# Four graph layers over 128 small graphs on one core: double-width instructions, the middle norm folded into G, scores spread by a repeated column, and new step orders

## The chip, the cores and the metric

One NeuronCore of a Trainium2 chip runs the whole program. The metric is device microseconds of one execution. Engines are named as in the profile: PE (TensorE), DVE (VectorE), ACT (ScalarE), POOL (GpSimd), SP (the queue that issues the DMAs).

## The reference, cut to what matters

`x` is [128 graphs, 128 nodes, 256], `adj` is [128, 128, 128], about a quarter of it nonzero. Every layer starts with a layer norm over the 256 features and a relu, and adds its result to `x`:

```
H = (adj != 0);  w = adj's first row;  Dn = 1/(H w);  Be = 1/(column sums of H)        # layer 0, hypergraph, 256 -> 512 -> 256
conv(v, W) = Dn * H @ (Be * (H^T @ (v @ W^T))) + b
x += conv(layer_norm(relu(conv(h, W1))) * gamma + beta, W2) + h
A = max(H, I);  dinv = rsqrt(row sums of A)                                             # layer 1, GCN
x += tanh(dinv * A @ (dinv * h) @ W + b)
s = (h @ w) @ a;  E = exp(leaky(8 * tanh((s_i + s_j) / 8)));  E *= adj                  # layer 2, attention
x += (E / rowsum(E) * rowsum(adj)) @ h @ w
x += adj @ (relu(adj @ (relu(adj @ h @ W1 + b1)) @ W2 + b2)) @ W3 + b3                  # layer 3, three GCN steps
```

## The kernel before, in words

The 128 graphs are worked in 16 passes (`GROUPS`). In a pass four streams A to D each hold J = 2 graphs. Each engine runs a list of steps per pass, `run` at L185, in an order made from the slot tables at L48 to L64: a table gives each step a place, stream B's steps stand a quarter of a pass after A's, C's a quarter after B's, and so on; a step whose place exceeds a pass is carried out in the next turn of the engine's loop (`back` = -1). So the steady state repeats the same pattern every quarter of a pass, with the streams rotated. Every engine works its list strictly in order; semaphores carry the dependences. The loop over passes is a hardware loop on each engine (`Fori`, L198).

Each layer is two kinds of products. A **U step** (`unit`, L300: 0U, 1U, 2U, 3U, 4U, 5U, 6U) multiplies by the graph's matrix (G for layer 0, AT for the GCN, AE for the attention, T = adj transposed for layer 3), in fp32, 128 columns at a time. ACT copies the result to UHI, rounded to fp32r (`take`, L375, step of the same name), and DVE forms the remainder ULO = U - UHI (`low`, L577). A **W step** (`weigh`, L315: 0W to 6W) multiplies by the weights, which are also split: per chunk of 128 features ULO x WHI, UHI x WLO, UHI x WHI, all fp32r, 256 columns wide (512 in 0W). Both graphs of a stream are handled by a loop over `j`: own PSUM bank, own instruction on ACT and DVE, own count on the semaphore. In 4W and 5W a first product adds the bias: SHARES (64 rows) x BIAS (64 rows), L329.

U steps and G and 3S rotate over two pairs of PSUM banks (`UB`), W steps over two pairs (`WB`); `bank_free` at L282 makes PE wait until the step that had the bank is read out.

The other steps that matter here:
- P, PT, P2 (DVE, L535 to L575): statistics of X, HT = (adj^T != 0) with counts, degrees from R = adj, and the small reciprocals after G. G = HT x [BHT | weights | 1] (`g_and_sums`, L336).
- 0W on DVE (`hidden`, L587) scales and adds the bias into Z (512 wide), ACT takes relu (L441), 0N gathers statistics of Z, POOL makes scale and shift, and ACT applies both to Z (0Z, `hidden_scale`, L446) before 1U.
- A norm is `stats` on DVE (L523: two `bn_stats`, a sum at L531, two `bn_aggr`), `norm` on POOL (L710: four or five instructions on 2 columns, one of them a power, L717) and `normalise` on ACT (L384).
- Attention: node scores on DVE (2S, L617), then ACT and DVE make the high and low part of a diagonal matrix of the scores (2D, L429 and L626), PE multiplies ones by it (3S, L345), ACT takes tanh and exp (L421, L436), DVE leak, product with T and row sums (L635 to L653).
- POOL: AT from HT (L727), the rest RES = TMP + X + B2 + H (L743, three instructions per graph), 2A (L766), X3 (L783).
- SP: X of the next pass is loaded after `rest_ready`, T and R after `p6U` (L213 to L224), outputs are stored after `c6W`.

Of the kernel before, what the change touches and what calls it, by code (L numbers as in the profile page):

```python
# [6 lines left out]
F32 = mybir.dt.float32  # L32
# [6 lines left out]
HALF = 32  # L39
TINY = 1.1754944e-38  # L40

PE_SLOTS = {  # L48
    "G": 2.890, "0U": 3.256, "0W": 3.665, "1U": 4.986, "1W": 5.422, "2U": 7.425, "2W": 7.801, "3S": 9.193,
    "3U": 9.672, "3W": 10.446, "4U": 11.122, "4W": 11.483, "5U": 12.384, "5W": 12.888, "6U": 13.845, "6W": 14.116}  # L50
ACT_SLOTS = {
# [3 lines left out]
DVE_SLOTS = {  # L55
# [3 lines left out]
POOL_SLOTS = {  # L59
    "P": 2.7, "AT": 6.2, "DI": 3.3, "R": 4.6, "0N": 5.2, "1W": 7.1, "2A": 8.4, "2X": 8.9, "2S": 9.5, "3W": 11.3,  # L60
    "X3": 12.8}
SP_SLOTS = {
    "X": -0.8, "T": 0.8, "O": 13.2}
SLOTS = 12  # L64


def ordered(slots):


    entries = []  # L70
# [10 lines left out]
def program(nc, xs, adj_t, adj_r, w1t, w2t, l1w, l2w, l2wt, l3w1, l3w2, l3w3,  # L81
            cols, b1, b2, l1b, l3b1, l3b2, l3b3, out):
# [6 lines left out]
    with ExitStack() as ctx:  # L89
# [744 lines left out]
```

## Time and profile before

| what | value |
|---|---|
| runs of the kernel | 1560.72, 1558.03 and 1559.4 us; median 1559.4 |
| profiled execution | span of its trace 1559.0 us; it has no separate time, so its span is its time here |
| busy: PE, DVE, ACT, POOL | 1491.9, 1429.5, 1156.2, 1048.1 us |
| granted TensorE clock, mean | 0.996 of full speed |
| DMA | 35 GB/s over the span, 10.9% of the 16 engines' time |

Reading it: the profile cuts the span in 40 slices, and apart from the first and last the slices look alike, because 16 equal passes run in a steady state. What a change is worth is therefore read in one quarter of a pass, multiplied by four and by the passes, with the start and the end looked at by themselves.

### The profile page before, as it was taken

The numbers are of one execution on the slowest core, as the hardware profiler recorded it, in microseconds if no ns is written. First come the engines' busy times: TensorE is split into PE (matmuls) and PEld (weight loads), VectorE is DVE, ScalarE is ACT, GpSimd is POOL, SyncE is SP. The second block draws the span as 40 slices with busy tenths as digits, with TensorE's granted clock in tenths as the row PEclk, the third lists the DMA queues.
The fourth block names the chain that finished last, engine by engine and source line by source line (L and its number), as shares of the span: only waits on it lengthen the run. The fifth ranks groups of instructions, "written<-read, shape, count | busy, mean of one in ns | idle before, by whom it ended". The sixth has DMA issues, their size and how long they took to land. (4 is left out here: it accounts for less than half of the span.)

```text
span 1559.0 us, 38399 instructions
## 1 busy us (share of the span) xinstructions
PE 1491.9 (96%) x10892; PEld 1369.1 (88%) x10892; DVE 1429.5 (92%) x5145; ACT 1156.2 (74%) x3080; POOL 1048.1 (67%) x2387
## 2 busy tenths in 40 slices
PE   5799999999999999999999999999999999999997
PEld 4798898998989989888988989989899898889896
DVE  6899899999999989999999999999899999999995
ACT  4677777777777777777777777777777787777774
POOL 3767666766767767677676667667677676766762
PEclk8999999999999999999999999999999999999999
DMA  4001101101101001011011011011011010110100
GB/s 152 1 29 35 42 27 34 41 24 37 38 23 41 34 28 41 28 34 41 27 34 41 27 34 41 27 34 41 21 41 34 27 41 28 34 41 27 34 21 21
DMA packets 39119, 54.76 MB, mean 35 GB/s; under 512 B 4464, under 2 KB 21488, under 8 KB 39024
## 3 DMA queue, kind: packets, MB, share of 16 engines
q1 hardware_dynamic: 39024, 53.89, 10.9%
q14 instruction: 84, 0.69, 0.1%
q8 instruction: 11, 0.18, 0.0%
HBM read 37.10 MB, written 16.78 MB: 35 GB/s over the span
## 5 line engine op out<-in xcount | busy, mean ns | idle before, releaser
L381 ACT ACTIVATE UHI_D<-UB 128x256 fp32r<-128x256 f32 (+1 forms) x224 | 91.0, 414 | 48.0 <-PE UB L310 40.6
L381 ACT ACTIVATE UHI_B<-UB 128x256 fp32r<-128x256 f32 (+1 forms) x224 | 90.8, 414 | 48.2 <-PE UB L310 43.4
L381 ACT ACTIVATE UHI_A<-UB 128x256 fp32r<-128x256 f32 (+1 forms) x224 | 90.6, 413 | 48.1 <-PE UB L310 42.8
L381 ACT ACTIVATE UHI_C<-UB 128x256 fp32r<-128x256 f32 (+1 forms) x224 | 90.8, 414 | 46.5 <-PE UB L310 41.9
L582 DVE TENSOR_TENSOR ULO_D<-UB,UHI_D 128x256 fp32r<-128x256 f32 (+1 forms) x224 | 93.4, 450 | 12.7 <-ACT UHI_D L381 12.6
L582 DVE TENSOR_TENSOR ULO_A<-UB,UHI_A 128x256 fp32r<-128x256 f32 (+1 forms) x224 | 93.8, 450 | 7.1 <-ACT UHI_A L381 7.1
L582 DVE TENSOR_TENSOR ULO_C<-UB,UHI_C 128x256 fp32r<-128x256 f32 (+1 forms) x224 | 93.7, 450 | 3.8 <-ACT UHI_C L381 3.7
L582 DVE TENSOR_TENSOR ULO_B<-UB,UHI_B 128x256 fp32r<-128x256 f32 (+1 forms) x224 | 93.9, 450 | 3.6 <-ACT UHI_B L381 3.3
L714 POOL TENSOR_TENSOR LN_D<-MV_D,EPS 128x2 f32<-128x2 f32 x80 | 15.6, 194 | 87.6 <-DVE MV_D L533 87.6
L714 POOL TENSOR_TENSOR LN_B<-MV_B,EPS 128x2 f32<-128x2 f32 x80 | 15.6, 195 | 83.8 <-DVE MV_B L533 83.8
L714 POOL TENSOR_TENSOR LN_A<-MV_A,EPS 128x2 f32<-128x2 f32 x80 | 15.6, 195 | 81.8 <-DVE MV_A L533 81.8
L714 POOL TENSOR_TENSOR LN_C<-MV_C,EPS 128x2 f32<-128x2 f32 x80 | 15.6, 195 | 71.9 <-DVE MV_C L533 71.9
L388 ACT ACTIVATE H_D<-RES_D,NB_D,LN_D 128x256 f32<-128x256 f32 x96 | 52.2, 593 | 5.0 <-POOL NB_D L722 2.9
L717 POOL TENSOR_TENSOR LN_A<-LN_A,MHALF 128x2 f32<-128x2 f32 x80 | 55.6, 695 | 0.2 <-issue 0.2
L717 POOL TENSOR_TENSOR LN_C<-LN_C,MHALF 128x2 f32<-128x2 f32 x80 | 55.7, 696 | 0.0
L717 POOL TENSOR_TENSOR LN_D<-LN_D,MHALF 128x2 f32<-128x2 f32 x80 | 55.6, 695 | 0.0
L717 POOL TENSOR_TENSOR LN_B<-LN_B,MHALF 128x2 f32<-128x2 f32 x80 | 55.6, 695 | 0.0
L750 POOL TENSOR_TENSOR RES_D<-TMP_D,X_D 128x256 f32<-128x256 f32 x32 | 23.7, 763 | 46.4 <-ACT TMP_D L407 46.4
L388 ACT ACTIVATE H_A<-RES_A,NB_A,LN_A 128x256 f32<-128x256 f32 x96 | 52.2, 594 | 3.4 <-POOL NB_A L722 1.3
L388 ACT ACTIVATE H_C<-RES_C,NB_C,LN_C 128x256 f32<-128x256 f32 x96 | 52.1, 591 | 3.2 <-POOL NB_C L722 1.1
L388 ACT ACTIVATE H_B<-RES_B,NB_B,LN_B 128x256 f32<-128x256 f32 x96 | 52.2, 594 | 2.3
L310 PE MATMUL UB<-T_A,H_A 128*128 128x128 f32 x384 | 51.6, 277 | 1.2 <-ACT H_A L388 1.2
(503 smaller groups left out, 7050.1 us busy)
## 6 DMA issues: line engine op xcount, KB each, us to landing
X_A<-in_xs SPq DMA_DIRECT2D x16, 256.0 KB, 2.6
X_B<-in_xs SPq DMA_DIRECT2D x16, 256.0 KB, 2.6
X_C<-in_xs SPq DMA_DIRECT2D x16, 256.0 KB, 2.7
X_D<-in_xs SPq DMA_DIRECT2D x16, 256.0 KB, 2.8
out_rows<-O_A SPq DMA_DIRECT2D x16, 256.0 KB, 2.0
out_rows<-O_B SPq DMA_DIRECT2D x16, 256.0 KB, 2.1
out_rows<-O_C SPq DMA_DIRECT2D x16, 256.0 KB, 2.1
out_rows<-O_D SPq DMA_DIRECT2D x16, 256.0 KB, 2.0
```

Source lines behind the costliest of these rows:

```text
L310: last = nc.tensor.matmul(bank(s, step, j)[:, m * P:(m + 1) * P], lhs(s, j)[:, m * P:(m + 1) * P], rhs(s, j), start=True, stop=True)
L381: nc.scalar.activation(dst[s][:, j, 0:n], bank(s, step, j)[:, 0:n], ACT.Copy).then_inc(sem(f"c{step}"), 1)
L388: nc.scalar.activation(H[s][:, j, :], src[s][:, j, :], ACT.Relu, bias=NB[s][:, j:j + 1], scale=LN[s][:, RSTD, j:j + 1]).then_inc(sem(done), 1)
L582: nc.vector.tensor_tensor(ULO[s][:, j, 0:n], bank(s, step, j)[:, 0:n], UHI[s][:, j, 0:n].bitcast(F32), ALU.subtract)\
L714: nc.gpsimd.tensor_tensor(LN[s][:, VE, :], MV[s][:, :, 1], EPS[:, :], ALU.add).then_inc(sem("ve" + tag), J)
L717: nc.gpsimd.tensor_tensor(rstd, LN[s][:, VE, :], MHALF[:, :], ALU.pow).then_inc(sem("rstd" + tag), J)
L750: nc.gpsimd.tensor_tensor(RES[s][:, j, :], TMP[s][:, j, :], X[s][:, j, :], ALU.add)\
```

## The change

It does the following.

1. **One instruction for both graphs** where operands allow: `take` and `low` of 0U and 2U to 6U, relu of 4W and 5W, G's copy, the attention's leak, exp and product with T, the last sum, and POOL's AT, RES, B2, H and L3B3 steps (constants are read through a repeated dimension, `pair`). Per-graph scalars still need an instruction per graph. Most semaphores count once per stream and pass instead of twice.
2. **PSUM**: 0W and 1U rotate over two double banks (WIDE), all other steps over four single banks that hold both graphs (BANK).
3. **W steps** on PE: for each graph first UHI x WLO and UHI x WHI, which need ACT's copy alone, then ULO x WHI, behind a second wait. The bias of 4W and 5W is one product, 128 rows by 512 columns, instead of two of 64 rows by 256.
4. **Middle norm folded**: at set-up W2 (times gamma) is centred (its column mean subtracted, three or four more matmuls and four DVE instructions), so the mean of Z drops out; the scale 1/std of the rows goes onto G (GZ, 128 wide per graph on ACT) instead of onto Z (512 wide). POOL's norm of z has two instructions.
5. **Scores**: 2H and 2L split the scores as two columns; 3S is four products of 128 columns whose stationary operand is one score column repeated 128 times and whose moving operand is the identity. The 128x128 diagonals on ACT and DVE are gone. Leak and exp are written to the PSUM bank of 3S, and DVE reads the exps from there.
6. **Front steps**: a separate copy TF of adj^T for HT, own loads for the first row (128x2 single elements into BHT) and the diagonal of adj (single elements), R loaded after `rr_ready` and X after `rest_x`. The degree comes from G's row of counts plus (diagonal == 0). H of layer 0 has its own tensor H0. There are seven DMAs per stream and pass where there were four.
7. **New orders**: all slot tables are new, many steps are cut in smaller ones (T, TC, TB, X, XA, DA to DD, S and A for each norm, 3I, 3J), with other steps between an instruction and the one that reads its result.

The new order on PE, one quarter of a pass (the sign - marks a step of the pass before): A5U- B3U- C2W- A5W- AG B3W- D1U- A6U- D1W- A6W- A0U B4U- C3S- A0W B4W- D2U-, and then the same with B for A and so on. On DVE: A4U- B3L- AT AX B3R- ATC B3E- D0W- ATB AXA C2U- D0S- A5U- D0A- C2W- B3U- ADA B3I- ADB C2S- ADC B3J- C2A- B3W- B3S- D1U- B3A- A6U- C2N- C2H- D1W- C2L- D1S- ADD D1A- A6W- A0U.

The diff, cut to its core (the old slot tables stand in the listing of the kernel):

```diff
+PERIOD = 88.0
 PE_SLOTS = {
+    "G": 5.35, "0U": 12.31, "0W": 15.06, "1U": 28.24, "1W": 29.30, "2U": 37.53, "2W": 47.58, "3S": 58.05,
+    "3U": 67.04, "3W": 71.77, "4U": 79.22, "4W": 81.45, "5U": 88.19, "5W": 92.43, "6U": 94.56, "6W": 97.75}
 ACT_SLOTS = {
+    "B": 7.76, "G": 9.11, "H0": 19.41, "0U": 20.10, "SH": 27.67, "0W": 29.48, "0Z": 35.13, "1U": 38.55,
+    "1W": 50.06, "2U": 50.52, "2W": 52.65, "2X": 62.96, "3T": 66.43, "R": 66.74, "3E": 70.56, "3U": 74.63,
+    "3W": 85.75, "4U": 88.17, "4W": 94.08, "5U": 95.60, "5W": 104.13, "6U": 105.95}
 DVE_SLOTS = {
+    "T": 1.35, "X": 1.84, "TC": 2.52, "TB": 3.72, "XA": 3.92, "DA": 7.12, "DB": 7.63, "DC": 8.09, "DD": 16.85,
+    "0U": 19.97, "0W": 24.84, "0S": 27.11, "0A": 27.54, "1U": 32.14, "1W": 36.20, "1S": 38.08, "1A": 40.42,
+    "2U": 47.94, "2W": 50.48, "2S": 51.69, "2A": 52.99, "2N": 56.85, "2H": 56.91, "2L": 59.70, "3L": 66.92,
+    "3R": 68.47, "3E": 68.78, "3U": 72.60, "3I": 73.27, "3J": 74.81, "3W": 75.32, "3S": 75.46, "3A": 78.04,
+    "4U": 88.72, "5U": 93.48, "6U": 100.06, "6W": 107.35}
 POOL_SLOTS = {
+    "N0": 23.21, "DI": 32.53, "RX": 35.58, "RB": 43.38, "NZ": 46.54, "RH": 50.72, "AT": 51.59, "N1": 53.29,
+    "2A": 68.84, "N2": 70.77, "2S": 75.24, "N3": 94.85, "X3": 99.95}
...
+        WIDE = [ctx.enter_context(nc.psum_tensor(f"WIDE{n}", [P, J, 512], F32)) for n in range(2)]
+        BANK = [ctx.enter_context(nc.psum_tensor(f"BANK{n}", [P, 512], F32)) for n in range(4)]
+        WIDE_STEPS = ("0W", "1U")
+        WIDE_TURNS = [x for x in PE_ORDER if x[1] in WIDE_STEPS]
+        BANK_TURNS = [x for x in PE_ORDER if x[1] not in WIDE_STEPS]
+        def bank(s, step):
+            turns, banks = (WIDE_TURNS, WIDE) if step in WIDE_STEPS else (BANK_TURNS, BANK)
+            return banks[[x[:2] for x in turns].index((s, step)) % len(banks)]
...
+            def load_first_row(s, group, n):
+                if n is not None:
+                    sp.wait_ge(sem("pG"), n)
+                sp.dma_start(BHT[s][:, :, P:P + 1], adj_t[group, STREAMS.index(s), :, :, 0:1], allow_slow_non_contiguous=True)\
+                    .then_inc(sem("first_row_loaded", s), 16)
+            def load_diagonal(s, group, n):
+                if n is not None:
+                    sp.wait_ge(sem("deg_ready"), n)
+                rows = adj_r[group, STREAMS.index(s)]
+                diagonal = bass.AP(rows.tensor, rows.offset, [[J * P + 1, P], [P, J], [1, 1]])
+                sp.dma_start(DIAG[s][:, :].unsqueeze(2), diagonal, allow_slow_non_contiguous=True)\
+                    .then_inc(sem("diagonal_loaded", s), 16)
...
+                    pe.wait_ge(sem(f"c{step[0]}U"), c["v"][0] if step == "1W" else c["n1"])
+                    bank_free(s, step, k)
+                    to = bank(s, step)
+                    biased = step in BIAS
+                    if biased:
+                        nc.tensor.matmul(to[:, :], SHARES[:, :], BIAS[step][:, :, :], start=True, stop=False)
+                    for j in range(J):
+                        dst = to[:, j, :] if step == "0W" else to[:, j * n:(j + 1) * n]
+                        at = [j * chunks * P + m * P for m in range(chunks)]
+                        if step == "1W" and j:
+                            pe.wait_ge(sem("c1U"), c["v"][j])
+                        for w in (lo, hi):
+                            for m in range(chunks):
+                                nc.tensor.matmul(dst, UHI[s][:, at[m]:at[m] + P], w[:, m, :],
+                                                 start=(w is lo and m == 0 and not biased), stop=False)
+                        if step == "1W":
+                            pe.wait_ge(sem("l1U"), c["v"][j])
+                        elif j == 0:
+                            pe.wait_ge(sem(f"l{step[0]}U"), c["n1"])
+                        for m in range(chunks):
+                            last = nc.tensor.matmul(dst, ULO[s][:, at[m]:at[m] + P], hi[:, m, :], start=False,
+                                                    stop=(m == chunks - 1 and (j == J - 1 or not biased)))
...
+                pe.wait_ge(sem("scores_split"), c["n1"])
+                bank_free(s, "3S", k)
+                for j in range(J):
+                    for part in (SHI, SLO):
+                        last = nc.tensor.matmul(bank(s, "3S")[:, j * P:(j + 1) * P], part[s][:, j:j + 1].to_broadcast([P, P]),
+                                                IDENTR[:, :], start=(part is SHI), stop=(part is SLO))
+                last.then_inc(sem("p3S"), 1)
...
+            def take(step):
+                def f(s, c, k):
+                    act.wait_ge(sem(f"p{step}"), c["n1"])
+                    nc.scalar.activation(UHI[s][:, 0:J * D], bank(s, step)[:, :], ACT.Copy).then_inc(sem(f"c{step}"), 1)
+                return f
...
+            def scale_g(s, c, k):
+                act.wait_ge(sem("lnz_ready"), c["n1"])
+                for j in range(J):
+                    nc.scalar.activation(GZ[s][:, j, :], G[s][:, j, 0:P], ACT.Copy, scale=LN[s][:, RSTD, j:j + 1])\
+                        .then_inc(sem("gz_ready"), 1)
...
+            def scores_tanh(s, c, k):
+                act.wait_ge(sem("s8_ready"), c["n1"])
+                act.wait_ge(sem("p3S"), c["n1"])
+                for j in range(J):
+                    last = nc.scalar.activation(AE[s][:, j, :], bank(s, "3S")[:, j * P:(j + 1) * P], ACT.Tanh,
+                                                bias=ST[s][:, S8, j:j + 1], scale=0.125)
+                last.then_inc(sem("scores_tanh"), 1)
+            def scores_exp(s, c, k):
+                act.wait_ge(sem("scores_leak"), c["n1"])
+                to = bank(s, "3S")[:, 0:J * P]
+                nc.scalar.activation(to, to, ACT.Exp, scale=8.0).then_inc(sem("e_ready"), 1)
...
+                for m in range(HC):
+                    last = nc.vector.scalar_tensor_tensor(W2[:, m, :], SETUP[:, 1, 0:D], -1.0 / DH, W2G[:, m, :], ALU.mult, ALU.add)
+                last.then_inc(sem("w2c_ready"), 1)
...
+                dve.wait_ge(sem("diagonal_loaded", s), c["dma"])
+                dve.wait_ge(sem("cG"), c["n1"])
+                nc.vector.tensor_scalar(ST[s][:, DNM, :], DNS[s], TINY, None, ALU.max).then_inc(sem("dnm"), 1)
+                nc.vector.scalar_tensor_tensor(ST[s][:, DG1, :], DIAG[s][:, :], 0.0, DGH[s], ALU.is_equal, ALU.add)\
+                    .then_inc(sem("deg_ready"), 1)
...
+            def leak(s, c, k):
+                dve.wait_ge(sem("scores_tanh"), c["n1"])
+                nc.vector.scalar_tensor_tensor(bank(s, "3S")[:, 0:J * P], AE[s][:, :, :], LEAK, AE[s][:, :, :], ALU.mult,
+                                               ALU.max).then_inc(sem("scores_leak"), 1)
...
+                dve.wait_ge(sem("t_loaded", s), c["dma"])
+                dve.wait_ge(sem("e_ready"), c["n1"])
+                nc.vector.tensor_tensor(AE[s][:, :, :], bank(s, "3S")[:, 0:J * P], T[s][:, :, :],
+                                        ALU.mult).then_inc(sem("ae_ready"), 1)
...
+                pool.wait_ge(sem("rest_x"), c["n1"])
+                nc.gpsimd.tensor_tensor(RES[s][:, :, :], RES[s][:, :, :], pair(B2[:, :]), ALU.add).then_inc(sem("rest_b2"), 1)
...
```

## Rows read from the trace of the kernel before

**Rows 1.** The page, busy time by engine, and granted clock in 40 slices.
```profile
PE 1491.9 (96%) x10892; PEld 1369.1 (88%) x10892; DVE 1429.5 (92%) x5145; ACT 1156.2 (74%) x3080; POOL 1048.1 (67%) x2387
PEclk8999999999999999999999999999999999999999
```

**Rows 2.** Windows of one quarter pass each: length, busy us by engine, clock, DMA.
```profile
594.00:617.24 23.24, 23.01 (x172) 21.21 (x172) 22.34 (x83) 17.86 (x48) 16.31 (x38) 1.00 0.10 34
617.24:640.48 23.24, 23.02 (x173) 21.22 (x172) 22.36 (x83) 17.90 (x49) 16.09 (x37) 1.00 0.11 34
```

**Rows 3.** Line 678, the last DVE step: durations ns, first and last start.
```profile
L678 DVE TENSOR_TENSOR O_A<-WB,RES_A x32: 389/410/417, 95.2 to 1511.4; 128x256 f32<-128x256 f32 x32
L678 DVE TENSOR_TENSOR O_D<-WB,RES_D x32: 405/410/425, 165.0 to 1556.1; 128x256 f32<-128x256 f32 x32
```

**Rows 4.** Timeline of PE: start us, us, instruction [idle before it <- releaser].
```profile
690.83 0.39 PE L350 MATMUL UB<-UHI_D,ONESR 128*128 128x256 f32 x1 [0.22 <-DVE ULO_D L631]
...
701.43 0.28 PE L331 MATMUL WB<-WHI2W,ULO_A 128*128 128x256 f32 x1
...
702.87 1.05 PE L310 MATMUL UB<-T_C,H_C 128*128 128x128 f32 x8
...
710.90 0.38 PE L331 MATMUL WB<-BIAS4W,SHARES 64*128 64x256 f32 x1
...
713.25 0.61 PE L342 MATMUL UB<-BHT_C,HT_C 128*128 128x130 f32 x4
714.08 0.39 PE L350 MATMUL UB<-UHI_A,ONESR 128*128 128x256 f32 x1 [0.23 <-DVE ULO_A L631]
...
714.42 1.05 PE L310 MATMUL UB<-G_C,H_C 128*128 128x128 f32 x8
...
716.45 0.40 PE L331 MATMUL WB<-WLO0W,UHI_C 128*128 128x512 f32 x1
716.68 0.40 PE L331 MATMUL WB<-WHI0W,UHI_C 128*128 128x512 f32 x1
```

**Rows 5.** Timeline of DVE and PE where the hardware loop turns.
```profile
645.40 0.49 DVE L639 SCALAR_TENSOR_TENSOR E_B<-E_B 128x128 f32<-128x128 f32 x2 [2.24 <-issue]
...
646.36 0.50 PE L331 MATMUL WB<-WHI0W,ULO_D 128*128 128x512 f32 x1 [1.42 <-DVE ULO_D L582]
```

**Rows 6.** Timeline of DVE: remainders 256 and 512 wide, each with the next.
```profile
605.94 0.72 DVE L582 TENSOR_TENSOR ULO_A<-UB,UHI_A 128x256 fp32r<-128x256 f32 x2
606.58 1.07 DVE L667 SCALAR_TENSOR_TENSOR RES_D<-WB,ST_D,RES_D 128x256 f32<-128x256 f32 x2
...
611.92 0.69 DVE L582 TENSOR_TENSOR ULO_B<-UB,UHI_B 128x512 fp32r<-128x512 f32 x1 [0.20 <-ACT UHI_B L381]
612.53 0.74 DVE L528 BATCH_NORM_STATS2 BN_A<-RES_A 128x6 f32<-128x256 f32 x2
```

**Rows 7.** ACT's copies by form: count, busy us, mean ns.
```profile
L381 ACT ACTIVATE UHI_A<-UB 128x256 fp32r<-128x256 f32 x192 | 71.4, 381 | 41.0 <-PE UB L310 35.7
L381 ACT ACTIVATE UHI_A<-UB 128x512 fp32r<-128x512 f32 x32 | 19.2, 600 | 7.1 <-PE UB L310 7.1
```

**Rows 8.** Timelines of DVE and POOL: DVE's two-input steps, and POOL's beside them.
```profile
600.18 1.49 POOL L750 TENSOR_TENSOR RES_B<-TMP_B,X_B 128x256 f32<-128x256 f32 x2 [0.94 <-ACT TMP_B L407]
...
601.00 0.81 DVE L651 SCALAR_TENSOR_TENSOR JUNK<-E_D,R_D 128x128 f32<-128x128 f32 x1
...
617.95 1.47 POOL L787 TENSOR_TENSOR RES_D<-RES_D,L3B 128x256 f32<-128x256 f32 x2
617.99 1.58 DVE L631 SCALAR_TENSOR_TENSOR ULO_A<-IDENT,ST_A,UHI_A 128x128 fp32r<-128x128 f32 x2
...
641.10 0.60 DVE L631 SCALAR_TENSOR_TENSOR ULO_B<-IDENT,ST_B,UHI_B 128x128 fp32r<-128x128 f32 x2
```

**Rows 9.** DMA issues: what, KB each, median us from issue to landing.
```profile
X_D<-in_xs SPq DMA_DIRECT2D x16, 256.0 KB, 2.8
...
L3B<-in_l3b SPq DMA_DIRECT2D x3, 128.0 KB, 8.1
```

More of the change, by code:

```diff
@@ L203, in run @@
                     loop[s, back]["dma"] = dma[back]
+                    loop[s, back]["v"] = [eng.snap(len(STREAMS) * J * k + J * done_at(s, back) - J + j + 1) for j in range(J)]
                 for s, step, back in order:
@@ L309, in f @@
-                        for m in range(chunks):
-                            last = nc.tensor.matmul(bank(s, step, j)[:, m * P:(m + 1) * P], lhs(s, j)[:, m * P:(m + 1) * P],
-                                                    rhs(s, j), start=True, stop=True)
-                        last.then_inc(sem(f"p{step}"), 1)
-                return f
+                        if rows is not None:
+                            pe.wait_ge(sem(rows), c["v"][j])
+                        if j == 0:
+                            bank_free(s, step, k)
@@ L375, in _, with high, high_rest, normalise @@
         def _(act):
-            def take(step, dst, n):
+            def high(step, name, value):
+                act.wait_ge(sem(name), value)
+                nc.scalar.activation(WHI[step][:, :, :], RAW[step][:, :, :], ACT.Copy).then_inc(sem("weights_high"), 1)
+            def high_rest():
+                for step in W_STEPS[2:]:
+                    high(step, "weights_loaded", 5 * 16)
+            def normalise(src, dst, ready, done):
                 def f(s, c, k):
+                    act.wait_ge(sem(ready), c["n1"])
@@ L379, in f @@
                     for j in range(J):
-                        act.wait_ge(sem(f"p{step}"), c["v"][j])
-                        nc.scalar.activation(dst[s][:, j, 0:n], bank(s, step, j)[:, 0:n], ACT.Copy).then_inc(sem(f"c{step}"), 1)
-                return f
-            def normalise(s, c, src, waits, done):
+                        nc.scalar.activation(dst[s][:, j, :], src[s][:, j, :], ACT.Relu, bias=LN[s][:, NB, j:j + 1],
+                                             scale=LN[s][:, RSTD, j:j + 1]).then_inc(sem(done), 1)
@@ L467, in high @@
-            def high(steps, waits, value):
-                act.wait_ge(sem(waits), value)
-                for step in steps:
-                    nc.scalar.activation(WHI[step][:, :, :], RAW[step][:, :, :], ACT.Copy).then_inc(sem("weights_high"), 1)
-            high(("0W",), "w1_loaded", 16)
-            run(act, ACT_ORDER, parts, {("A", "0U"): lambda: high(("1W",), "w2g_ready", HC),
-                                        ("A", "0W"): lambda: high(W_STEPS[2:], "weights_loaded", 5 * 16)})
+                    act.wait_ge(sem(f"p{step}"), c["n1"])
@@ L487, in spread @@
                 last.then_inc(sem("spread_ready"), 1)
[L489 to L499 removed]
+                dve.wait_ge(sem("ident_ready"), 1)
@@ L515, in last_weights @@
+                last.then_inc(sem("bias_high"), 1)
+                dve.wait_ge(sem("bias_high"), 1)
                 for step, row in (("4W", L3B1), ("5W", L3B2)):
-                    lower = BIAS[step][HALF:2 * HALF, :]
-                    nc.vector.tensor_tensor(lower, row[HALF:2 * HALF, :], lower.bitcast(F32), ALU.subtract)
+                    for j in range(J):
+                        rest = BIAS[step][P // 2:P, j, :]
+                        nc.vector.tensor_tensor(rest, row[P // 2:P, :], rest.bitcast(F32), ALU.subtract)
```

667 lines of the change are left out of this document (315 added, 352 removed), and 6 rows, old and new, of tables (ACT_SLOTS, DVE_SLOTS).

## The prediction

> **What bounds the kernel now.** I read the page first, then single quarters of a pass, then the steps inside one. The page shows PE busy 96% and DVE 92%, at full clock after the first slice [rows 1]. A steady quarter is 23.24 us long; PE is busy for 23.0 of it, DVE for 22.3, ACT for 17.9, POOL for 16.3 [rows 2]. The same step of PE returns after 714.08 - 690.83 = 23.25 us, and the only idle time on PE between is the 0.23 us before the score products, which wait for DVE's diagonal [rows 4]. So PE sets the pace, and DVE is so close behind that it would take over if it alone kept its work.
>
> The first outputs of stream A are written at 95.2 us and the last at 1511.4: 15 passes of 94.41 us [rows 3]. Four quarters are 92.96, so each pass loses 1.45 us once. That is where DVE's loop turns: it stands still for 2.24 us with nothing to wait for, its remainder for 0W is late, and PE idles 1.42 us [rows 5]. The profiled execution is thus 95.2 (head) + 15 x 94.41 + 47.6 (from A's last output to the end of the 1559.0 us span). The median of the runs is 0.4 us above that execution; I add the 0.4 at the end. A difference under about 0.2% (3 us) could not be told from no change.
>
> **The change on PE, per quarter.**
> - Biases of 4W and 5W. 2W takes 702.87 - 701.43 = 1.44 us for twelve products (0.12 each). 4W takes 713.25 - 710.90 = 2.35 with two more of 64 rows, so these cost 0.91 [rows 4]. They become one product of 512 columns; such a product costs 716.68 - 716.45 = 0.23 [rows 4]. Gain 0.68 in 4W and the same in 5W: -1.36. If a new bias product cost as much as an old one (0.46), the gain would be 0.90.
> - Wait before 3S: its cover is now a split of two columns, and the PE order puts 6U to 4U between. -0.23.
> - G: 0.83 until the next start, less the 0.23 of waiting, is 0.60 for four instructions; in a row of their kind they take 0.11 each (eight in 703.76 - 702.87 = 0.89, where the next step starts) [rows 4]. One wait fewer between: -0.12.
> - 3S: today two products of 256 columns, 0.34 (714.42 - 714.08) [rows 4]. Then four of 128 columns, which no row shows in fp32r. Low end: the 0.11 of a pass of fp32, 0.44. High end: fp32 needs two such passes per product, 0.89. I take 0.48, four at the 0.12 of rows 4, since today's fp32r product of 256 columns costs no more than its weight load: +0.14.
> - Four changes from fp32 to fp32r in the new order against five, 0.08 us each (3W, after a U step, takes 1.52 where 2W takes 1.44): -0.08. An estimate from the same stretch of PE's timeline.
> - New tight place. After 4W only 2U (0.86) stands before 5U of the same stream, where the old order had G, 3S and 0U. The relu must fit: its operand is complete 0.16 after the last issue (a product lasts 0.28 and the next starts after 0.12 [rows 4]), and a 512-wide copy on ACT takes 0.60 [rows 7], 0.78 with the signals. It fits by under 0.1, and ACT must just be free. +0.10.
> - All other products stay, in number and width. The new second wait inside a W step costs nothing if the remainder is there: the step runs 0.48 us on UHI first. If it is late, PE stands as it would have before.
>
> Sum: 23.24 - 1.36 - 0.23 - 0.12 + 0.14 - 0.08 + 0.10 = 21.69 us.
>
> **The others must stay under that.** *DVE:* a pair of 256-wide remainders holds DVE 606.58 - 605.94 = 0.64 us, one of 512 holds it 0.61 [rows 6]; pairing in itself gives next to nothing, six times 0.03. What counts is what goes: the diagonal, 1.58 us beside POOL and 0.60 without [rows 8]; the row sums, up to 0.81 each, which now read the exps from PSUM; the sum in each of five norms, two 128-wide degree passes, and the stalls between dependent small steps, which now have other work between. I estimate 22.3 - 1.2 (diagonal less its two small successors) - 0.9 (row sums) - 1.9 (sums, degrees, pairs, gaps) = 18.3 us, with contention as today. *ACT:* two copies of 0.38 become one of 0.60 [rows 7], about -0.2 for each of eight steps; 0Z shrinks from 512 to 128 columns: some 15 us. *POOL:* same elements, 1.49 us per pair [rows 8], about 16.5 us. All have 3 us or more to spare.
>
> *Queues.* In the PE order I followed each in-order chain. PE has 12 us of other work from 2W to 3S of a stream, and that chain (0.8 output, 0.7 tanh, 1.5 POOL add, norm 2.3, relu 1.1, scores 1.4) takes about 8.5. From 1W to 2U there are 8.3 for about 5; from 3S to 3U 6.3 for about 3.5, with POOL's queue behind. Each step four bank turns back is one that the new step's own chain has already needed, so the four single banks add no wait. These are estimates from the durations in such timelines.
>
> *SP.* Seven DMAs per stream for four, three more instructions on a queue that is idle most of the time. F, W, X and D are placed about a quarter pass or more before their readers. The single-element ones have no row. Between the 2.8 us of a 256 KB load and the 8.1 us of the slowest start-up load [rows 9], any value is covered by over 20 us. Their waits (pG, deg_ready, rest_x) are long past in the order. Cost nothing; if the cover were gone, 5 us per quarter at most.
>
> *Loop turn.* DVE stands 2.24 us in each pass still; more counts are kept per turn, so perhaps 2.7. It now comes between D0U and A4U, where the remainder of 4U has about 3 us. Then C2U and B3U follow late. DVE's slack of 3 us per quarter recovers it. Lower end 0.5, upper end 2.4; I keep today's 1.45.
>
> Pass: 4 x 21.69 + 1.45 = 88.2 us; 15 passes 1323.
>
> **Head and tail.** Head: the work on PE is less, but DVE's first weights now wait for W2, the centring adds four DVE instructions and four products, and A's 6W stands about 4 us later in the order: 95.2 + 2. Tail: chains of single steps, where a 512-wide copy and remainder take longer than two that overlap, while PE starts on UHI early: 47.6. Total 97.2 + 1323 + 47.6 = 1467.8, with 0.4 for the median **1468 us**.
>
> **Rivals.**
> 1. *Contention makes DVE the bound (slower).* The second row-sum step, 128 columns, started at 601.00 and lasted 0.81, until just after POOL's pair (600.18 + 1.49) ended; both diagonals of A ended with POOL's pair as well, while B's, with no such step on POOL, took 0.60 for two [rows 8]. So a DVE step with two SBUF inputs waits until the running POOL instruction is done. The change doubles these POOL instructions to about 1.45. Eight steps per quarter on DVE stay of this kind (2N twice, 3L, 2L, 3J, DA, DC, DD). If each waited half of 1.45 more than today, 5.8 us, DVE would take 24.1, a pass 4 x 24.1 + 2.2 = 98.6, the whole 97 + 1479 + 48 = 1624 us. It decides from about 5 us of added waiting per quarter; beyond that it is slower than before. Against: POOL runs such instructions under half of the time, and the worst waiters (diagonal, row sums) leave the set. The Trainium skill, page SBUF - State Buffer, section "SBUF: two separate sides", states this as an exclusive lock held for the whole instruction; by that rule longer POOL instructions make each wait longer, and the trace agrees with the 0.81. Chance 8%.
> 2. *The orders don't fit.* One chain is late by 1 us per quarter on PE, for instance the relu before 5U or the scale of G before 1U, which comes after G's copy in ACT's queue with under 1 us to spare. 22.7 x 4 + 2.2 = 93.0, total 1540; half of that, 1503. For: many waits are now a single one for both graphs, so work starts later. Chance 19% for 1508 to 1555.
> 3. *The change doesn't do on PE what the sum says*: the new bias product costs as much as the old ones, and 3S comes at its high end. That would give 21.69 + 0.41 + 0.46 = 22.56, 91.7 per pass, 1520. Both ends together are unlikely; one alone gives about 1495, within my range. No change at all, 2%.
>
> The Trainium skill, page TensorE: Matmul & The Clock Gate, section "Back-to-back issue gap", gives about 81 ns for a sustained pair of load and product at 128 columns. No row here shows one; by it 3S would be 0.32 and the total some 10 us lower.
>
> **How the numbers follow.** Forecast case, 1440 to 1508: 69%. Rival 2 19%, rival 3 beyond the range 2%, rival 1 8%, no change 2%. The low end has loop turn 0.5, no relu wait and 3S by its low end: 21.55 x 4 + 0.5 = 86.7, 1301 + 144 = 1445. The high end is one unknown at its worst and some waiting, 1510. Faster by over 0.2%: 0.90, within 0.2% 0.02, slower 0.08.
>
> **What would show it.** Right: PE's steady quarter near 21.7 us with busy time as long; 4W and 5W near 1.75; DVE busy 18 to 20 of it; the copy of 512 columns 0.60; 3S under 0.5. Wrong: the idle time on PE with releaser ACT H (relu) or ACT GZ, or DVE two-input steps of over 1 us ending with POOL's, or 3S near 0.9.

## The result, and the profile after

The changed kernel takes **1435.4 us** (median of 4 runs, 1433.5 to 1436.0) where the kernel before takes 1559.3 in the runs beside it: a ratio of 0.920 [0.919, 0.922]. The forecast was 1468 and the range began at 1445, so the direction was right and the time came out 33 us lower, 10 below the range.

The page of the changed kernel: busy time and instructions by engine, the granted clock in 40 slices, and the queue that fetches instructions (packets, MB, share).

```profile
PE 1392.3 (97%) x10900; PEld 1331.7 (93%) x10900; DVE 1287.9 (90%) x4001; ACT 990.5 (69%) x2312; POOL 947.7 (66%) x1876
...
PEclk9999999999999999999999999999999999999999
...
q14 instruction: 11, 0.09, 0.0%
```

Against [rows 1], DVE executes 4001 instructions for 5145 and PE is busy 1392 us for 1492. The last line has a counterpart on the page of before that I did not use:

```profile
q14 instruction: 84, 0.69, 0.1%
```

The windows of the changed kernel's four quarters of one pass, as [rows 2]:

```profile
615.49:637.14 21.65, 21.65 (x173) 20.73 (x171) 20.21 (x63) 15.42 (x36) 14.69 (x29) 1.00 0.16 42
637.14:658.67 21.53, 21.53 (x173) 20.61 (x172) 20.18 (x63) 15.41 (x36) 14.70 (x29) 1.00 0.15 43
658.67:679.79 21.12, 21.12 (x172) 20.50 (x171) 19.25 (x63) 15.26 (x36) 14.97 (x29) 1.00 0.16 44
679.79:701.45 21.66, 21.66 (x173) 20.78 (x172) 20.23 (x63) 15.42 (x36) 14.65 (x29) 1.00 0.15 42
```

PE is busy for all of each. Three quarters last 21.6 us and one 21.1, and in that one DVE is busy 1 us less; both will matter. The last step of stream A, as [rows 3]:

```profile
L692 DVE TENSOR_TENSOR O_A<-BANK,RES_A x16: 682/684/685, 100.0 to 1389.1; 128x512 f32<-128x512 f32 x16
```

The profiled execution (span 1433.8 us) is 100.0 + 15 x 85.94 + 44.7. Forecast were 97.2, 88.2 and 47.6: the head was 2.8 longer, the tail 2.9 shorter, and the 15 passes 2.26 us shorter each. That is the whole miss.

PE's timeline, to compare with [rows 4]: the score products, 4W with its bias, then the starts of 2W, 5W, G and the step behind it in the same quarter, and the same four in the short quarter.

```profile
617.19 0.30 PE L384 MATMUL BANK<-IDENTR,SHI_C 128*128 128x128 f32 x1
...
617.66 0.68 PE L365 MATMUL WIDE<-WLO0W,UHI_A 128*128 128x512 f32 x2
...
620.51 0.39 PE L357 MATMUL BANK<-BIAS4W,SHARES 128*128 128x512 f32 x1
620.74 0.40 PE L365 MATMUL BANK<-WLO4W,UHI_B 128*128 128x256 f32 x2
...
622.13 1.05 PE L330 MATMUL BANK<-AT_D,H_D 128*128 128x128 f32 x8
...
624.78 0.48 PE L365 MATMUL BANK<-WLO2W,UHI_D 128*128 128x256 f32 x2
...
626.39 0.39 PE L357 MATMUL BANK<-BIAS5W,SHARES 128*128 128x512 f32 x1
...
628.18 0.61 PE L315 MATMUL BANK<-BHT_B,HT_B 128*128 128x130 f32 x4
...
628.75 0.47 PE L365 MATMUL BANK<-WLO3W,UHI_C 128*128 128x256 f32 x2
...
667.94 0.48 PE L365 MATMUL BANK<-WLO2W,UHI_B 128*128 128x256 f32 x2
...
669.39 0.39 PE L357 MATMUL BANK<-BIAS5W,SHARES 128*128 128x512 f32 x1
...
671.04 0.61 PE L315 MATMUL BANK<-BHT_D,HT_D 128*128 128x130 f32 x4
671.40 0.37 PE L365 MATMUL BANK<-WLO3W,UHI_A 128*128 128x256 f32 x1
```

3S takes 617.66 - 617.19 = 0.47 us, the bias 0.23, 4W 622.13 - 620.51 = 1.62 (it was 2.35), G 0.36 in the short quarter and 0.57 in the other (it was 0.60 and a wait of 0.23). 2W takes 626.39 - 624.78 = 1.61 us and 5W 628.18 - 626.39 = 1.79 in the first, 1.45 and 1.65 in the short one.

Then DVE's waits in the kernel before: line waited at, what it waited for, us in total, times, longest.

```profile
DVE E_B L639 <- issue: 33.0, 14, 2.5
DVE ULO_D L582 <- ACT UHI_D L381: 12.6, 24, 3.0
```

The first is the standstill at the loop turn of [rows 5], 14 times. In the changed kernel there is no such row; its longest entries are waits for ACT. This is the step behind its loop turn, the remainder of A's 4U:

```profile
682.40 0.69 DVE L599 TENSOR_TENSOR ULO_A<-BANK,UHI_A 128x512 fp32r<-128x512 f32 x1 [0.20 <-ACT UHI_A L444]
```

### The profile page after: what moved, and what is told of

Same layout as the page of the kernel before. It is cut to its first block, busy times and chain, and to the rows that moved or that the text cites. A ratio compares the mean times of both kernels' runs of the same rounds, so it can differ in the third digit from the quotient of the medians.

```text
span 1433.8 us, 34585 instructions
## 1 busy us (share of the span) xinstructions
PE 1392.3 (97%) x10900; PEld 1331.7 (93%) x10900; DVE 1287.9 (90%) x4001; ACT 990.5 (69%) x2312; POOL 947.7 (66%) x1876
## 4 chain that ended last, share of the span: by engine, by line
PE 95%; DVE 2%; ACT 1%; issue 0%; DMA 0%; POOL 0%; SPq 0%; DVEq 0%; POOLq 0%
PE BANK L365 29%; PE BANK L330 24%; PE BANK L372 15%; PE WIDE L365 8%; PE WIDE L341 8%; PE WIDE L372 4%; PE BANK L357 2%; PE BANK L315 2%; PE BANK L384 2%; DMA TMP_D<-in_l2wt 0%; PE WIDE L278 0%; DVE BN_B L550 0%; DVE BN_C L550 0%; ACT UHI_D L444 0%; PE WIDE L284 0%
## 5 line engine op out<-in xcount | busy, mean ns | idle before, releaser
L444 ACT ACTIVATE UHI_B<-BANK 128x512 fp32r<-128x512 f32 x96 | 57.0, 593 | 43.9 <-PE BANK L330 43.9
L444 ACT ACTIVATE UHI_D<-BANK 128x512 fp32r<-128x512 f32 x96 | 57.1, 595 | 41.1 <-PE BANK L330 41.1
L444 ACT ACTIVATE UHI_C<-BANK 128x512 fp32r<-128x512 f32 x96 | 57.0, 594 | 41.0 <-PE BANK L330 41.0
L444 ACT ACTIVATE UHI_A<-BANK 128x512 fp32r<-128x512 f32 x96 | 57.1, 594 | 39.1 <-PE BANK L330 39.1
L599 DVE TENSOR_TENSOR ULO_D<-BANK,UHI_D 128x512 fp32r<-128x512 f32 x96 | 65.2, 680 | 18.7 <-ACT UHI_D L444 18.0
L599 DVE TENSOR_TENSOR ULO_A<-BANK,UHI_A 128x512 fp32r<-128x512 f32 x96 | 65.2, 680 | 12.3 <-ACT UHI_A L444 11.8
L599 DVE TENSOR_TENSOR ULO_C<-BANK,UHI_C 128x512 fp32r<-128x512 f32 x96 | 65.1, 678 | 11.1 <-ACT UHI_C L444 9.3
L599 DVE TENSOR_TENSOR ULO_B<-BANK,UHI_B 128x512 fp32r<-128x512 f32 x96 | 65.7, 684 | 10.4 <-ACT UHI_B L444 8.5
L330 PE MATMUL BANK<-T_D,H_D 128*128 128x128 f32 x384 | 52.0, 278 | 1.6 <-ACT H_D L484 1.4
L413 ACT ACTIVATE H_D<-RES_D,LN_D 128x256 f32<-128x256 f32 x96 | 52.0, 590 | 1.9 <-POOL LN_D L744 1.9
```

Of the source, the lines that this page charges most:

```text
L330: last = nc.tensor.matmul(bank(s, step)[:, at:at + P], lhs[s][:, j, m * P:(m + 1) * P], rhs(s, j), start=True, stop=True)
L413: nc.scalar.activation(dst[s][:, j, :], src[s][:, j, :], ACT.Relu, bias=LN[s][:, NB, j:j + 1], scale=LN[s][:, RSTD, j:j + 1]).then_inc(sem ...
L444: nc.scalar.activation(UHI[s][:, 0:J * D], bank(s, step)[:, :], ACT.Copy).then_inc(sem(f"c{step}"), 1)
L599: nc.vector.tensor_tensor(ULO[s][:, 0:J * D], bank(s, step)[:, :], UHI[s][:, 0:J * D].bitcast(F32), ALU.subtract).then_inc(sem(f"l{step}"), 1)
```

## Experiments

**1. Is the standstill at the loop turn the fetching of code?** In before's steady pass five packets of the instruction queue fall, about 8 KB each: two beside the loop turn and three some 32 us apart. The changed kernel has three in the 1220 us from 110 to 1330. By the program's list, DVE's loop has 390 instructions before and 318 after. Four kernels move the changed loop by putting one-column copies in front of it, outside the loop:

```diff
+            for i in range(55):    # 105, 125, 211 in the others
+                nc.vector.tensor_copy(FILL[:, i:i + 1], ONES[:, 0:1])
             run(dve, DVE_ORDER, parts, ...
```

> The changed kernel, with 55 one-column copies of DVE into a spare tile ahead of everything, outside the loop; the loop itself is not touched. Theory (code fetch): the before trace has about five instruction-fetch packets in each pass and the changed one has none between its first and its last pass, because before's loop on DVE (390 instructions in the compiled stream) does not stay in DVE's instruction memory and the changed one's (318) does. From where the packets fall in the pass I place the blocks at 128 instructions; 55 more in front push the loop across one block more. So the packets come back, several tens of them in the whole run, DVE stands still about 2 us at its loop turn again, and the run takes 5 to 22 us longer (15 passes, up to 1.45 us each as before; less, since DVE has 1.4 us of slack per quarter now). Rival (register work, or the standstill was only uncovered by before's order): copies in front change nothing: no packets, pass 85.94 us, the time within 0.2% of the changed kernel's 1435.4 (1433 to 1438).

> The same with 105 copies in front. If block boundaries are what counts, this moves the loop on to the next block, where it again fits: no packets per pass, pass 85.9 us, 1434 to 1440 us, faster than with 55 copies although it does more. If it is the total length of the program or the copies themselves that cost, it is slower than with 55 copies. Rival (register work or order): as the changed kernel, like the other.

Measured: **1474.3 us with 55 copies and 1538.3 with 105** (the changed kernel: 1435.4). Both have 82 packets for 11. The waits of DVE, with 55 copies and then with 105:

```profile
DVE ULO_A L600 <- issue: 43.5, 14, 3.1
```

```profile
DVE ULO_A L600 <- issue: 82.4, 14, 6.2
```

The passes last (1428.1 - 100.8) / 15 = 88.49 us and (1490.7 - 100.8) / 15 = 92.66, against 85.94. So fetching is the cause, and neither my bound of 22 us nor my choice of 105 held. With 55 copies the quarter with the turn takes 23.55 us of PE and the others 21.70. The turn's quarter is thus 1.85 longer than its neighbours; another 0.6 comes from these, as the changed kernel has a quarter of 21.1 just ahead of the turn's and here all three last 21.70. PE's third product group of 4W waits at the turn for DVE's remainder:

```profile
613.90 0.28 PE L366 MATMUL BANK<-WHI4W,UHI_A 128*128 128x256 f32 x1
614.69 0.51 PE L373 MATMUL BANK<-WHI4W,ULO_A 128*128 128x256 f32 x2 [0.39 <-DVE ULO_A L600]
```

With 105 copies DVE stands 5.91 us at the turn, as if two blocks in a row were missing, and the quarter takes 664.45 - 636.59 = 27.86 us (from the bias of 4W to the next). From this the loop's start had to lie a few instructions ahead of a block boundary. DVE's step behind the turn, the PE step that waits for it, and PE's window just after (columns as in [rows 2]):

```profile
639.90 0.69 DVE L600 TENSOR_TENSOR ULO_A<-BANK,UHI_A 128x512 fp32r<-128x512 f32 x1 [5.91 <-issue]
...
640.65 0.79 PE L373 MATMUL BANK<-WHI4W,ULO_A 128*128 128x256 f32 x2 [3.20 <-DVE ULO_A L600]
...
641.00:646.00 5.00, 4.99 (x23) 4.72 (x23) 5.00 (x18) 3.79 (x9) 3.00 (x5) 0.50 0.00 0
```

Not all of this run's price is fetching. After its wait of 3.20 us PE works at a granted clock of 0.50, the lower level of 1.2 GHz, until about 647. The mean granted clock is 0.971 in all four runs of this kernel, where it is 0.995 with 55 copies. By these means (an estimate) some 0.024 x 1535 = 37 of the 103 us over the changed kernel are the lower clock.

> The changed kernel with 125 copies in front instead of 105. My revised reading of the two runs before: DVE keeps four blocks of 128 instructions, one of them being fetched ahead, so a loop stays in it only if it touches three blocks; with 105 copies the loop began a few instructions ahead of a boundary (5.9 us of standstill, two fetches in a row), with 55 in the middle of a block (3.1 us, one fetch). Twenty more copies put the start just behind the boundary, the 318 instructions touch three blocks, and all is gone: no packets per pass, pass 85.9 us, 1434 to 1440 us. Rival (the cost grows with what stands ahead of the loop): 55 cost 39 us and 105 cost 103 us, so 125 cost 103 to 130 us, over 1538 us.

**1443.8 us**, 12 packets, no wait named "issue" on DVE. Twenty more copies make it 94.5 us faster, the clock's part included. Experiment 4 comes back to the 8 us by which it stays above the changed kernel.

> The changed kernel with 211 copies in front. It tells apart two readings that fit all runs so far. Reading 1: DVE's instruction memory is four blocks of 128, one of them always being fetched ahead, and a loop stays only if it touches three; 211 copies put the start in the last part of a block (as 105 and 55 did), the loop touches four, so the packets (about 80) and a standstill of about 3 us per pass come back: pass 88 to 89 us, 1470 to 1490 us. Reading 2: two blocks of 256, and a loop stays if it touches two; 211 copies put it well inside two: no packets per pass, no standstill, pass 86.0 to 86.4 us, 1435 to 1455 us (the copies themselves may delay the first pass by up to 12 us).

**1484.9 us**, 83 packets, the standstill back:

```profile
DVE ULO_A L600 <- issue: 43.0, 14, 3.1
```

The pass is (1438.0 - 108.5) / 15 = 88.63 us; stream A's first output comes 8.5 us later for the copies. Reading 1 stands in what it says of the loop: the five runs fit if code comes in blocks of 128 instructions and a loop stays only if it touches three. For a loop of 318 they then place the unmoved start 12 to 22 instructions behind a block boundary. With blocks of 256, of which two are kept, the first four runs would place it 140 to 150 behind one; 211 copies would move it to 95 to 105, where 318 instructions fit, and yet the packets came back. Whether DVE holds four blocks and fetches one ahead, or holds three, no run here tells. The Trainium skill, page Advanced Engine Details and Errata, section "ISA Cache", has lines of 256 instructions and two of them; the run with 211 copies disagrees with a loop being kept as long as it touches two such lines. The Trainium skill, page Runtime: NRT & Kernel Launch, section "Instruction fetch mechanics", warns of a stall at a taken branch out of the window, which these runs show with its price.

**2. The same in the kernel before.** Its 390 instructions can't fit in three blocks of 128, so the loop was cut to 362, and the same loop run at two places. Both kernels leave out the row sum of exp times adjacency and take the reciprocal of the member count in its place, so they don't compute the attention as the reference has it; at 1W and 6W two waits per graph became one per stream:

```diff
-                for j in range(J):
-                    dve.wait_ge(sem("e_ready"), c["v"][j])
-                    nc.vector.scalar_tensor_tensor(JUNK[:, j, 1, :], E[s][:, j, :], 1.0, R[s][:, j, :], ...,
-                                                   accum_out=ST[s][:, RSA, j:j + 1]).then_inc(sem("rsa"), 1)
...
-                dve.wait_ge(sem("rsa"), c["v"][J - 1])
-                nc.vector.reciprocal(ST[s][:, RSA, :], ST[s][:, RSA, :]).then_inc(sem("rsa_inv"), J)
+                nc.vector.reciprocal(ST[s][:, RSA, :], ST[s][:, CNM, :]).then_inc(sem("rsa_inv"), J)
...
```

> The kernel before with its loop on DVE cut from 390 to 362 instructions, so that it can fit at all, and 98 copies in front that put it just behind a block boundary. Left out of the computation: the sum of exp times adjacency over a row (the reciprocal is taken of the member count instead); two waits per graph are made once per stream. By the theory of blocks there are no packets per pass, no standstill of 2.24 us, and a pass is four quarters of 23.2 us, 93.0 instead of 94.4: about 1537 us for the whole. Rival (the 1.45 us per pass came from somewhere else than code): standstill as before, the same time as its twin with 43 copies, 1555 to 1560 us.

> The twin of the kernel with 98 copies: the same loop, cut in the same way (the row sum of exp times adjacency left out), with 43 copies in front, so that the loop touches four blocks. By the theory of blocks it has about five packets per pass and a standstill of 2 to 3 us at each turn, and is 20 to 40 us slower than its twin. Rival: no difference between the two beyond 3 us.

With 98 copies **1524.3 us** (I had expected 1537) and 15 packets; with 43 **1557.4** and 84. The waits with 43 copies; with 98 there is no "issue" among DVE's longest.

```profile
DVE E_B L642 <- issue: 32.3, 14, 2.5
```

Same loop, same work, 33.1 us apart, passes of (1472.3 - 94.1) / 15 = 91.88 and (1507.8 - 93.4) / 15 = 94.29 us. On PE the quarter with the turn takes 24.77 us with 43 copies, 1.5 above its neighbours (23.25), as in the full kernel; with 98 copies it takes 22.71, and the neighbours 23.07. So without the fetch the turn's quarter is 2.06 us shorter and each of the others 0.18, 2.4 per pass where I had read 1.45 from the neighbours. Why the turn's quarter then falls below its neighbours, no run here shows. Whether the full kernel would gain the same 2.4 wasn't tried, as its loop can't be made to fit without leaving work out.

**3. The bias products, term by term.** The old form put back into the changed kernel, and a form that changes the width but keeps the rows (with 64 rows the factor in SHARES and the rows of BIAS change with it, not shown):

```diff
-                    if biased:
-                        nc.tensor.matmul(to[:, :], SHARES[:, :], BIAS[step][:, :, :], start=True, stop=False)
                     for j in range(J):
+                        if biased:    # [0:P // 2] in one kernel, [0:P] in the other
+                            nc.tensor.matmul(dst, SHARES[0:P // 2, :], BIAS[step][0:P // 2, j, :], start=True, stop=False)
```

> The changed kernel with the biases of 4W and 5W as they were: two products of 64 rows, 256 columns, one at the start of each graph's half, in place of one of 128 rows and 512 columns. By the first term of my sum an old bias product costs 0.46 us and the new one 0.23: 2 x 0.46 - 0.23 = 0.68 more in each of 4W and 5W, 1.36 per quarter, 16 passes of four quarters and PE at the bound in all but the ends: about +82 us, 1517 us. Rival (the gain came elsewhere, the products cost 0.12 each as their columns say): 1435 us.

> The changed kernel with two bias products of 256 columns each, but of all 128 rows. It tells what made the old ones dear. If it was the 64 rows, these cost 0.12 each, 0.23 together like the one of 512, and the time stays at 1435 us. If it was that each graph has a product of its own, they cost 0.46 each as before and it takes about 1517 us.

**1515.9 us with 64 rows** (+80.5; I had said +82) **and 1436.4 with 128**. PE's timeline with 64 rows, then with 128:

```profile
629.49 0.39 PE L362 MATMUL BANK<-BIAS4W,SHARES 64*128 64x256 f32 x1
629.80 0.51 PE L365 MATMUL BANK<-WLO4W,UHI_A 128*128 128x256 f32 x2
630.15 0.40 PE L365 MATMUL BANK<-WHI4W,UHI_A 128*128 128x256 f32 x2
630.38 0.40 PE L372 MATMUL BANK<-WHI4W,ULO_A 128*128 128x256 f32 x2
630.72 0.38 PE L362 MATMUL BANK<-BIAS4W,SHARES 64*128 64x256 f32 x1
```

```profile
620.00 0.28 PE L362 MATMUL BANK<-BIAS4W,SHARES 128*128 128x256 f32 x1
620.11 0.40 PE L365 MATMUL BANK<-WLO4W,UHI_B 128*128 128x256 f32 x2
```

A product of 64 rows takes 0.31 to the next start, not 0.11, and slows both neighbours: the pair behind it takes 0.35 for 0.23, and it starts 0.34 behind the pair before it. So it is the 64 rows between products of 128 that cost, going in and coming out. Merging two products of 256 into one of 512 gives nothing: 0.23 us for either.

The same part alone in the kernel before:

```diff
-HALF = 32
+HALF = 64
...
```

> The kernel before with one part of the change alone: its bias products get 128 rows instead of 64 (256 columns each, as they are). A run of the changed kernel showed that such a product costs 0.12 us instead of 0.46, so PE's work falls by 1.36 us per quarter, to about 21.9 us. If PE alone set the pace before, the time falls by 62 x 1.36 = 84 us, to 1475 us. If DVE (22.3 us busy per quarter, with waits between dependent steps) takes over, the quarter ends at about 22.6 us and the time at 1520 us; then DVE's relief is what made the gain on PE count.

**1531.0 us**, 28 less instead of 84, and 11 above what I had put for DVE taking over. A pass is (1485.4 - 92.2) / 15 = 92.88 us, 1.5 shorter for 5.4 of work on PE. The page's busy line, and the longest waits of PE:

```profile
PE 1419.2 (93%) x10892; PEld 1349.7 (88%) x10892; DVE 1420.3 (93%) x5145; ACT 1137.9 (74%) x3080; POOL 1047.5 (68%) x2387
```

```profile
PE WB L331 <- DVE ULO_D L582: 32.5, 17, 2.4
PE UB L350 <- DVE ULO_D L631: 15.3, 16, 1.4
PE UB L350 <- DVE ULO_C L631: 14.8, 16, 1.0
PE UB L350 <- DVE ULO_A L631: 14.8, 16, 1.0
```

In three quarters of each pass PE now waits 1 us for the diagonal, where it waited 0.23, and in the fourth up to 2.4 at the turn. DVE was the second bound, as close as the prediction said: the same exchange is worth 28 us here and 80.5 in the changed kernel, where DVE has room. A small part of the missing 56 us is the clock: behind the longest of these waits (2.33 us, at 726.09) it was 0.50 for some 3 us, and over the run it is 0.990 to 0.992 where the kernel before has 0.996 to 0.998, by which I estimate 8 us. How DVE's relief divides among the paired instructions, the folded norm, the scores and the new orders isn't shown: no run undoes one of them alone.

**4. The lock between DVE and POOL (rival 1).** DVE and POOL of the changed kernel: the leak and the two-column maximum, each with the POOL instruction beside it; then the leak in the short quarter.

```profile
618.61 1.29 POOL L788 TENSOR_TENSOR RES_B<-RES_B,L3B 128x512 f32<-128x512 f32 x1
618.71 1.48 DVE L655 SCALAR_TENSOR_TENSOR BANK<-AE_C 128x256 f32<-128x256 f32 x1
...
621.57 1.28 POOL L763 TENSOR_TENSOR RES_A<-TMP_A,X_A 128x512 f32<-128x512 f32 x1 [1.67 <-ACT TMP_A L438]
621.59 1.28 DVE L570 TENSOR_SCALAR ST_B<-ST_B 128x2 f32<-128x2 f32 x1
...
661.89 0.42 DVE L655 SCALAR_TENSOR_TENSOR BANK<-AE_A 128x256 f32<-128x256 f32 x1
661.96 1.50 POOL L788 TENSOR_TENSOR RES_D<-RES_D,L3B 128x512 f32<-128x512 f32 x1
```

Whoever starts second waits for the whole instruction of the other: the leak lasts 1.48 us where it comes 0.1 behind POOL and 0.42 where it comes 0.07 ahead, and then POOL's lasts 1.50 for 1.29. The maximum, 128 x 2 elements, begins 0.02 behind POOL's addition and lasts 1.28, until that has ended. The Trainium skill, page SBUF — State Buffer, section "SBUF: two separate sides", says this of a DVE step with two SBUF inputs or in its two-port mode. The trace agrees for the leak, which reads two inputs from SBUF, in both directions; the maximum has one input, and that it waits is shown, but not in which mode it runs. Two kernels try whether it reaches PE:

```diff
-    "T": 1.35, "X": 1.84, "TC": 2.52, ...
+    "T": 1.35, "X": 1.84, "TC": 1.90, ...
```

> The changed kernel with one step of DVE's order moved: the two-column maximum of the member counts (1.28 us in every quarter, where it starts 0.02 us behind POOL's 512-column addition and ends with it) goes ahead of the two row sums instead of behind them. My theory: it waits for the whole POOL instruction, and that is 1.1 us of DVE per quarter that also reaches PE: in three of four quarters the remainders for 2W and 5W come 0.1 to 0.3 us late (21.6 us), in the fourth, in which the leak on DVE happens not to meet POOL's addition (0.42 instead of 1.48), they don't (21.12). Moved by 0.5 us it escapes, the quarters all take about 21.1, the pass 84.5, and the time is 1412 us (1405 to 1425). Rival (PE is busy the whole time, so DVE's waits are free): 1433 to 1438 us, though DVE's busy time falls by 1 us per quarter. Second rival: the lock finds another victim, and nothing is gained on DVE either.

```diff
-                nc.gpsimd.tensor_tensor(RES[s][:, :, :], TMP[s][:, :, :], X[s][:, :, :], ALU.add).then_inc(sem("rest_x"), 1)
+                for j in range(J):
+                    last = nc.gpsimd.tensor_tensor(RES[s][:, j, :], TMP[s][:, j, :], X[s][:, j, :], ALU.add)
+                last.then_inc(sem("rest_x"), 1)    # and so for the three other additions
```

> The changed kernel with POOL's four 512-column additions made per graph again (eight of 256 columns), DVE's and PE's code untouched. This is what my first rival named: the doubled POOL instructions make DVE's waits longer. Theory: the two-column maximum falls from 1.28 to about 0.65 us, the leak from 1.48 to under 1, DVE is 1 to 1.5 us less busy per quarter, and the quarter of PE goes from 21.6 to about 21.2: 1415 to 1425 us. Rival (PE is the bound, DVE's waits are free): DVE's busy time falls, the time stays at 1433 to 1438 us.

**1416.9 us and 1415.9 us**: ratios to before of 0.909 and 0.908, both interval ends clear of the changed kernel's 0.920. All quarters are now short ones: 21.15 us, a pass of (1368.0 - 98.2) / 15 = 84.65 us with the early maximum. A window of the kernel with the early maximum, then of the one with split additions:

```profile
595.07:616.22 21.15, 21.15 (x172) 20.52 (x171) 19.07 (x63) 15.13 (x37) 14.66 (x29) 1.00 0.15 43
```

```profile
596.24:617.39 21.15, 21.15 (x173) 20.52 (x171) 19.10 (x64) 15.19 (x37) 15.39 (x33) 1.00 0.15 43
```

And the steps themselves (line, count, ns min/median/max). The maximum with the early place; the maximum and the leak with split additions:

```profile
L570 DVE TENSOR_SCALAR ST_B<-ST_B x16: 141/144/149, 24.4 to 1288.6; 128x2 f32<-128x2 f32 x16
```

```profile
L570 DVE TENSOR_SCALAR ST_B<-ST_B x16: 149/740/743, 24.7 to 1290.0; 128x2 f32<-128x2 f32 x16
...
L655 DVE SCALAR_TENSOR_TENSOR BANK<-AE_B x16: 423/923/924, 80.5 to 1351.2; 128x256 f32<-128x256 f32 x16
```

So a wait of DVE mattered though PE was "97% busy": in the long quarters of the changed kernel 2W takes 1.6 us for the short quarter's 1.45, 5W 1.8 for 1.65 and G 0.57 for 0.36, which shows as longer steps and not as idle time. In the kernel with 125 copies the leak meets POOL in all four streams (medians 1.48 to 1.54) and no quarter is a short one (21.5 to 21.7). Its pass is (1397.2 - 101.1) / 15 = 86.41, 0.47 over the changed kernel's: that is 7 of its 8 us.

> The early maximum and POOL's additions per graph together. Each alone took the time from 1435 to 1416 us and the quarter of PE to 21.15 us. If both worked by taking away the same lateness on PE, together they give no more than one: 1413 to 1418 us, with DVE another 1 us per quarter less busy. If each had taken away a part of its own, together they give about 1397 us.

**1416.0 us**: together no more than one alone, as the same lateness can go only once.

> The kernel with the early maximum, and 3U of one stream ahead of 5U of the other on PE, ACT and DVE. In the kernel with the early maximum the one PE step that still stands longer than its twins is 5U, 0.96 us where the same step 6U takes 0.81: it waits for the relu after 4W. With 3U between, the relu has 0.8 us more. Theory: 5U 0.81, quarter 21.0, 0.15 x 62 = 9 us less than the 1416.9 of the early maximum, 1408 us. Rival: 3U's operand comes 0.2 us or more late instead, or the remainder for 5W does, and it takes 1417 to 1430 us.

**1440.3 us**, 23 slower than with the early maximum alone. 5U fell to 0.81 as meant, but PE's group for the bias of 5W (xcount, busy, mean ns, idle) has a mean of 494 ns, where it is 396 in the changed kernel:

```profile
L357 PE MATMUL BANK<-BIAS5W,SHARES 128*128 128x512 f32 x64 | 31.6, 494 | 4.9 <-ACT UHI_D L444 0.7 <-ACT UHI_C L444 0.7
```

ACT's copy of 5U now comes right before 5W (649.38 to 649.97, 5W starts at 650.02), and 2W and 5W take 1.73 and 1.86 us for 1.46 and 1.65. This is the second part of my rival, operands of 5W coming late, and dearer than its 1430; the 0.15 us of 5U is the cheaper place to wait.

## Why the prediction was wrong, and where it was right

**The step that failed: "Loop turn. DVE stands 2.24 us in each pass still".** I took "nothing to wait for" to be the loop's keeping of counts, which the change adds to, and kept 1.45 us per pass (lower end 0.5). It was the fetching of DVE's code, and the change cut the loop to a length and put it at a place where it stays. The term is 0: 15 x 1.45 = 22 us of the 34 in the passes. The sentence "DVE's slack of 3 us per quarter recovers it" didn't hold either: where the fetch comes back, a pass is 2.55 us longer for 3.1 on DVE. That the loop stays is luck of place: begun 55 instructions further on, the same change brings 85 us instead of 124.

**PE's sum, 21.69 per quarter:** measured 21.65, 21.53, 21.66 and 21.12. The remaining 12 us of the miss are 4 x 21.69 - 85.96 = 0.80 per pass, mostly the short quarter. Term by term it was less exact than it looks. Biases: predicted 0.68 per step, 4W measured 2.35 - 1.62 = 0.73, the put-back test 80.5 us for 82. 3S: 0.48 predicted, 0.47 measured, so neither the 0.89 nor the 0.32 that the prediction also names. G: 0.48 predicted, 0.36 without waiting. The relu ahead of 5U: 0.10 predicted, 0.15 measured. Against the 21.15 of a quarter without the lateness of experiment 4 my sum is 0.5 too long, and that lateness fills just this gap: that three quarters agree with 21.69 within 0.2 is in part luck. 4W and 5W, which the prediction's last paragraph wanted near 1.75, take 1.6 and 1.65 to 1.81.

**DVE:** 18.3 us per quarter predicted, 20.2 measured. The step "with contention as today" failed: 1.1 us at the leak (3L, on rival 1's list of steps that wait) in three quarters of four, and 1.1 at the maximum (TC), which was not on that list. Copies of 512 columns on ACT: 0.60 predicted, 0.594 measured; ACT 15 and 15.4; POOL 16.5 and 14.7.

**Rival 1** was right as a mechanism and wrong in price: the two waits come to some 2 us per quarter, not 5.8, DVE stayed under PE, and they cost 18 to 19 us, not the 156 between its 1624 and my 1468. **Rival 2** did not come about as put; what was late came through the lock. Moving one step shows how near it was: 3U ahead of 5U costs 23 us. **Rival 3** fell: both products cost what the sum said.

**Head and tail:** 97.2 predicted, 100.0 measured; 47.6 and 44.7. I did not look into either; they cancel.

## What to carry to other kernels

A gap with no releaser just behind a loop's branch, repeated every pass, is a suspect for code fetching: look at the instruction queue's packets per pass, and test it by adding idle instructions in front of the loop, as here its place decided whether its code was fetched again. When such a test makes PE wait long, look at the granted clock too before you give the whole difference to the fetch. Where DVE and POOL work from SBUF side by side, a two-column step can last as long as POOL's longest instruction (1.28 us for 0.14 here); move the small step half a microsecond, or halve the large one. An engine at 97% busy may still be late in pieces of 0.1 us: compare the same step in several quarters before you call it the bound.

## What the runs showed of the hardware that I had not expected

- A loop turn that fetches its code holds DVE for 3.1 us (with 55 and with 211 copies), at one place 5.9; the same program takes 1443.8 us with 125 instructions in front of its loop and 1538.3 with 105.
- After a wait of 3.2 us (105 copies) PE's granted clock was 0.50 for over 6 us, where the 1.42 us of waiting at before's turn and the 1.3 us with 55 copies left it at 1.00.
- A product of 64 rows among products of 128 rows and the same width costs 0.31 us more (1515.9 - 1436.4 us over 256 such products).
- The lock acts both ways: POOL's addition took 1.50 us for 1.29 where DVE's leak began 0.07 ahead of it.
